# The scan's step-row fetches issued by ScalarE, next to the decay that frees their slot, with the positions of the steps set anew

## The chip, the cores and the metric

One core of one Trainium2 chip. The metric is the device time of one execution in microseconds (us). The kernel before took 2951.22 us (median of three runs, 2949.57 to 2960.09).

## What is computed

Two transformer layers with adaptive layer norm run over 32 samples of 256 tokens and 128 features. The reference, cut to what matters:

```python
# layer 0: attention with relative positions, then a mixture of 16 experts, 4 of them per token
x = x + ga * attention(layernorm(x) * (1 + ca) + sa)
x = x + gb * experts(layernorm(x) * (1 + cb) + sb)
# layer 1: a state-space layer (256 channels, 16 states), then three matrices and a tanh
dt  = softplus(dt_low @ W_dt + b_dt)
dA  = exp(dt[..., None] * A)                                  # [b, t, 256, 16]
dBx = dt[..., None] * B_ssm[:, :, None, :] * x_conv[..., None]
h   = associative_scan(h_t = dA_t * h_(t-1) + dBx_t)          # over t
y   = einsum('btdn,btn->btd', h, C_ssm)
x = x + ga * ((y * silu(z) + D * x_conv) @ W_out)
h = layernorm(x) * (1 + cb) + sb
x = x + gb * tanh(h @ W @ A1 @ A2 + bias)
```

## The kernel before

Two samples form a pair (512 tokens), and there are 16 pairs. Each pair passes through four stages: attention (32 chunks), experts (16), scan (32 batches of 128 rows of channel and state) and the last matrices. The stages of different pairs overlap. All engines walk through one list of steps, from FIRST to LAST; a pair begins every STEPS = 128 steps. The table `AT` says at which step of a pair each piece of work stands in its engine's program (the suffix names the engine, `_sync` is SyncE's DMA queue). Positions are only an order within one engine; between engines semaphores decide. So an engine that waits holds up whatever stands behind it in its own program. Attention's pieces return every 4 steps, an expert's every 8, and a scan batch m of a pair stands at SCAN + 27m//8, that is every 3.4 steps from step 388 on.

What a scan batch is made of, for the steps in question:

- The scan's step size and its product with x_conv are stored from SBUF (tile `step`) to the HBM tensor `dt_rows` (`s_store_sync`, L1072 to L1075). A fetch (L1105, "work<-dt_rows") reads 16 channels of it back, repeated over 8 groups of partitions, 128 x 1024 floats or 512 KB, into one of four slots of `ring`. There are 16 fetches a pair (n = 0 to 15), issued by SyncE in four groups of four. Each fetch serves two batches, four batches apart.
- ScalarE's decay (L1118, "bank<-work,neg_a") makes exp of the first half of a slot into the one PSUM bank 6; it waits for the fetch and for the scan before it, which frees the bank.
- GpSimd's input (L1129) multiplies the second half of the slot with a row of B, out of `bc`; VectorE scans (L1135); GpSimd reads out with C (L1142); TensorE sums over states (L1154).
- A slot is free when both the decay and the input of the second batch that uses it are done. SyncE waits for that at L1102 and L1103 and then issues the next fetch. `dt_rows` must have been stored (semaphores `dt_out`).

SyncE's one queue carries everything: besides the fetches the spread of the keys (L564, "ke<-ke"), the scatter of the queries (L553 and L556, many small pieces, "q_all<-q_rows"), the experts' weights (stored at L828 after ScalarE's copy at L821, fetched at L836 as "w_bc<-w_rows_d" for GpSimd's L902), the rows of B and C (stored at L1062, fetched at L1083), and the output (L1238, "out<-x_b"), whose buffer VectorE overwrites two pairs later at L927.

On ScalarE the attention's exp (L597, "probs") and copy of the turned probabilities (L615, "probs_t") and the experts' tanh (L878) stand between the decays. TensorE's L580 are the scores, L607 the turns, L870 and L871 an expert's gate, L889 its up and L907 its down product.

Of the kernel before, what the change touches and what calls it, by code (L numbers as in the profile page):

```python
# [15 lines left out]
PAIRS = B // 2  # L16
# [32 lines left out]
RING = 4  # L49
# [18 lines left out]
def build(nc, dram, out, q_rows, w_rows_d, dt_rows, bc_rows):  # L68
    ctx = ExitStack()
    with ctx:  # L70
# [254 lines left out]
        def tokens(ap):  # L325
# [8 lines left out]
        FIRST, LAST = -102, STEPS * (PAIRS - 1) + 538  # L334
# [3 lines left out]
            a_out_tensor=[79, 144], a_out_scalar=[79, 145], s_end_vector=[448, 500],  # L338
            a_spread_sync=[[-28, -28, -12, 4], [20, 36, 52, 68]], a_scatter_sync=[[-22, 4], [37, 69]], x_a_sync=-100,
            x_res_sync=104, a_store_sync=-35, m_store_sync=178, m_fetch_sync=-11, s_rows_sync=377,  # L340
            s_rows_in_sync=[378, 380, 384, 386], s_store_sync=[372, 374], s_fetch_sync=-14, f_store_sync=534,
            a_scores_tensor=0, m_gate_tensor=1, m_up_tensor=3, m_down_tensor=9, a_turn_tensor=5, a_values_tensor=40,
            a_inverse_tensor=42, s_sum_tensor=6, a_turned_tensor=-48, a_keys_tensor=-42, a_values_in_tensor=-37,
            a_query_tensor=-33, f_end_tensor=531, a_back_tensor=150, b_turned_tensor=159, m_logits_tensor=164,
            m_weights_tensor=178, m_back_tensor=326, s_turned_tensor=340, s_in_x_tensor=[348, 356], s_step_tensor=[364, 365],
            s_rows_tensor=374, s_in_z_tensor=[390, 397], f_out_tensor=508, f_back_tensor=513, f_turned_tensor=524,
            f_mix_tensor=527, s_decay_scalar=0, m_tanh_scalar=2, a_turn_scalar=8, a_exp_scalar=3, a_values_scalar=42,
            a_norm_scalar=-51, a_turned_scalar=-42, a_keys_scalar=-40, a_values_in_scalar=-35, a_query_scalar=-33,
            b_norm_scalar=156, b_turned_scalar=159, m_logits_scalar=166, m_weights_scalar=180, m_end_scalar=324,
            s_norm_scalar=340, s_turned_scalar=342, s_conv_scalar=[351, 359], s_step_scalar=[366, 366], s_rows_scalar=373,  # L350
# [743 lines left out]
        def last_batch_of(n):  # L1094
            return 8 * (n // 4) + 4 + n % 4

        def s_fetch_sync(sp, p, n):
            sp.wait_ge(dt_out[n // 8], (n // 8 + 1) * 16 * (p + 1))
            at = FETCHES * p + n - RING
            if at >= 0:  # L1100
# [594 lines left out]
```

## Time and profile before

| | us |
|---|---|
| median of three runs | 2951.22 |
| lowest and highest run | 2949.57, 2960.09 |
| the profiled execution's own time | 2962.1 |
| its span in the trace | 2960.3 |
| TensorE busy | 2429.2 (82%) |
| GpSimd busy | 1826.6 (62%) |
| VectorE busy | 1898.4 (64%) |
| ScalarE busy | 1633.4 (55%) |
| DMA packets' share of 16 engines | 51.9% |

Engines: PE is TensorE, PEld its weight loads, DVE VectorE, ACT ScalarE, POOL GpSimd, SP SyncE; SPq is SyncE's queue of DMA issues. The time of an issue in the timeline is how long the issuing instruction took, not the transfer. "a <-b" means that engine a sat idle until b. The span has a fill (to about 520 us), a stretch in which all four stages run side by side (560 to 2210 us is taken for it here, ten pairs), and a drain (from about 2450 us) in which the last pairs' scans are nearly alone.

### The profile page before, as it was taken

Reading aid. Unit: us, or ns where it says so; the run is one execution under the profiler, and the core shown is the slowest. Engines: PE = TensorE matmul, PEld = TensorE weight load, DVE = VectorE, ACT = ScalarE, POOL = GpSimd, SP = SyncE. Lnnn points to the kernel's source line nnn. Section 1 sums busy time; section 2 is a strip of 40 time slices with the busy share of each in tenths; the row PEclk is TensorE's granted clock in tenths of the full one; section 3 lists DMA queues with packets and bytes.
Section 4 is the critical chain, followed back from the end, with each engine's and each line's share of the span. In section 5 each row is a group of like instructions: output and inputs, shape, how many; then the busy total and the mean of one; then the engine's idle time right before and its main releaser. Section 6 shows DMA issues by size and latency. Waiting matters only on the chain.

```text
span 2960.3 us, 37054 instructions
## 1 busy us (share of the span) xinstructions
PE 2429.2 (82%) x9792; PEld 1231.4 (42%) x9792; DVE 1898.4 (64%) x3116; ACT 1633.4 (55%) x4152; POOL 1826.6 (62%) x2311
## 2 busy tenths in 40 slices
PE   2889988989898898989898888989898898867422
PEld 2555544444444444444444444444444444312100
DVE  2344557676767767676767767676767767565533
ACT  1655555656566666556566666666566656423322
POOL 2011248575767758575757767575758667675865
PEclk9999999999999999999999999999999999978655
DMA  5324355565655566565656655555656554434241
GB/s 123 45 44 73 57 123 99 118 109 120 114 100 122 102 131 104 112 106 118 115 109 114 106 122 111 115 109 109 118 111 119 106 112 94 115 86 109 70 108 43
DMA packets 495421, 304.95 MB, mean 103 GB/s; under 512 B 347258, under 2 KB 413738, under 8 KB 494762
## 3 DMA queue, kind: packets, MB, share of 16 engines
q1 hardware_dynamic: 495212, 302.58, 51.9%
q8 instruction: 82, 1.34, 0.2%
q14 instruction: 127, 1.03, 0.2%
HBM read 242.21 MB, written 26.74 MB: 91 GB/s over the span
## 4 chain that ended last, share of the span: by engine, by line
PE 37%; DVE 19%; issue 14%; POOL 11%; DMA 9%; ACT 7%; SPq 1%; DVEq 0%; ACTq 0%; POOLq 0%
PE bank L580 7%; DMA work<-dt_rows 7%; PE bank L889 6%; PE bank L871 4%; DVE work L1135 4%; POOL work L1142 4%; POOL work L1129 3%; PE bank L1154 3%; DVE zh L885 2%; PE bank L607 2%; PE bank L1007 2%; DVE step L981 2%; PE bank L907 2%; DVE nmax L587 2%; PE bank L682 2%
## 5 line engine op out<-in xcount | busy, mean ns | idle before, releaser
L1129 POOL TENSOR_TENSOR work<-work,bc 128x512 f32<-128x512 f32 x512 | 655.0, 1285 | 250.2 <-DMA work<-dt_rows 140.4
L1135 DVE TENSOR_TENSOR_SCAN work<-bank,work 128x512 f32<-128x512 f32 x512 | 621.7, 1214 | 215.1 <-POOL work L1129 161.6
L1142 POOL TENSOR_TENSOR work<-work,bc 128x512 f32<-128x512 f32 x512 | 659.1, 1293 | 115.5 <-DVE work L1135 113.8
L902 POOL TENSOR_TENSOR zh<-zh,w_bc 128x512 f32<-128x512 f32 x256 | 325.2, 1270 | 482.4 <-DVE zh L895 475.7
L1118 ACT ACTIVATE bank<-work,neg_a 128x510 f32<-128x510 f32 x512 | 353.0, 689 | 478.9 <-DVE work L1135 367.0
L597 ACT ACTIVATE probs<-bank,nmax 128x256 f32<-128x256 f32 x1024 | 474.9, 471 | 216.8 <-DVE nmax L587 215.9
L580 PE MATMUL bank<-ke,q_all 96*128 96x256 f32 x2048 | 560.9, 398 | 17.9 <-DMA q_all<-q_rows 17.9
L580 PEld LDWEIGHTS bank<-ke,q_all 96*128 96x128 f32 x2048 | 385.5, 198 | 227.2 <-issue 161.7
L587 DVE TENSOR_REDUCE nmax<-bank 128x2 f32<-128x512 f32 x512 | 347.1, 678 | 189.7 <-PE bank L580 180.1
L889 PE MATMUL bank<-h_b,w_t 128*128 128x512 f32 x512 | 299.4, 668 | 128.5 <-DVE zh L885 120.0
L607 PEld LDWEIGHTS bank<-ident,probs 128*128 128x128 f32 x2048 | 256.8, 146 | 287.1 <-issue 211.3
L607 PE MATMUL bank<-ident,probs 128*128 128x128 f32 x2048 | 323.2, 282 | 62.3 <-ACT probs_t L615 61.9
L615 ACT ACTIVATE probs_t<-bank 128x512 f32<-128x512 f32 x512 | 304.7, 595 | 98.5 <-PE bank L637 80.2
L885 DVE SCALAR_TENSOR_TENSOR zh<-th,bank 128x512 f32<-128x512 f32 x256 | 174.1, 680 | 220.8 <-ACT th L878 220.1
L895 DVE SCALAR_TENSOR_TENSOR zh<-bank,b_c,zh 128x512 f32<-128x512 f32 x256 | 190.9, 746 | 193.9 <-PE bank L889 192.6
L871 PE MATMUL bank<-h_b,w_t 128*128 128x512 f32 x512 | 310.6, 691 | 0.0
L907 PE MATMUL bank<-zh,w_t 128*128 128x512 f32 x512 | 282.9, 636 | 3.8 <-POOL zh L902 3.8
L878 ACT ACTIVATE th<-bank 128x512 f32<-128x512 f32 x256 | 152.3, 595 | 147.0 <-PE bank L871 144.2
L1154 PE MATMUL bank<-work,sel_d 128*32 128x512 f32 x1024 | 166.9, 689 | 77.5 <-POOL work L1142 77.5
L597 ACT ACTIVATION_READ_ACCUMULATOR probs<-bank,nmax 128x1 f32 x1024 | 206.9, 202 | 0.0
L889 PEld LDWEIGHTS bank<-h_b,w_t 128*128 128x128 f32 x512 | 81.1, 196 | 248.1 <-DVE zh L885 213.1
L907 PEld LDWEIGHTS bank<-zh,w_t 128*128 128x128 f32 x512 | 102.3, 203 | 146.4 <-issue 135.3
(190 smaller groups left out, 2509.1 us busy)
## 6 DMA issues: line engine op xcount, KB each, us to landing
work<-dt_rows SPq DMA_DIRECT2D x256, 512.0 KB
w_bc<-w_rows_d SPq DMA_DIRECT2D x256, 256.0 KB, 9.4
ke<-ke SPq DMA_DIRECT2D x128, 256.0 KB, 8.7
bc<-bc_rows SPq DMA_DIRECT2D x64, 256.0 KB
x_in<-in_x SPq DMA_DIRECT2D x32, 256.0 KB, 6.2
q_all<-q_rows SPq DMA_DIRECT2D x512, 8.0 KB
dt_rows<-step SPq DMA_DIRECT2D x16, 512.0 KB, 2.9
dt_rows<-step SPq DMA_DIRECT2D x32, 256.0 KB, 2.2
```

The lines of the kernel that those rows point to most:

```text
L580: last = nc.tensor.matmul(bank[n % 2][:, k * T:(k + 1) * T], q_all[0:QROWS, i0 + k, :], ke_q[:, i0 + k, :], start=True, stop=True)
L587: nc.vector.tensor_reduce(nmax[:, 2 * c:2 * c + 2], bank[n % 2][:, :].rearrange("p (k t) -> p k t", k=2), AX_X, ALU.max, negate=True).then ...
L597: last = nc.scalar.activation(probs[:, n % 2, k, :], bank[n % 2][:, k * T:(k + 1) * T], ACT.Exp, bias=nmax[:, i:i + 1], accum_out=rsum[:, ...
L607: last = nc.tensor.transpose(tile(bank[2], 2 * kh + k), probs[:, n % 2, k, kh * P:(kh + 1) * P], ident[:, :])
L871: nc.tensor.matmul(bank[4][:, :], w1_t[:, e, :], h_b[:, p % 2, :], start=False, stop=True).then_inc(m_g, 1)
L889: nc.tensor.matmul(bank[4][:, :], w3_t[:, e, :], h_b[:, p % 2, :], start=True, stop=True).then_inc(m_u, 1)
L902: nc.gpsimd.tensor_tensor(zh[:, n % 3, :], zh[:, n % 3, :], w_bc[:, n % WB, :], ALU.mult).then_inc(m_p, 1)
L907: nc.tensor.matmul(bank[5][:, :], w2_t[:, e, :], zh[:, n % 3, :], start=False, stop=(e == NE - 1)).then_inc(m_w2, 1)
L1118: nc.scalar.activation(segments(bank[6][:, :])[:, :, 1:], segments(ring[n % RING][:, 0, :])[:, :, 1:], ACT.Exp, scale=neg_a[:, SG * j + s: ...
L1129: nc.gpsimd.tensor_tensor(hb[at % HB], ring[n % RING][:, 1, :], bc[:, s, :], ALU.mult).then_inc(s_dbx, 1)
L1135: nc.vector.tensor_tensor_scan(hb[at % HB], bank[6][:, :], hb[at % HB], 0.0, ALU.mult, ALU.add).then_inc(s_h, 1)
L1142: nc.gpsimd.tensor_tensor(hb[at % HB], hb[at % HB], bc[:, SG + batch(m)[2], :], ALU.mult).then_inc(s_hc, 1)
```

## The change

SyncE no longer issues the fetches. ScalarE does, as `s_fetch_scalar`, with the same waits and the same transfer. In ScalarE's program the fetch for batch m stands at step 12 before that batch's decay, one or two steps behind the decay (of batch m - 4) that is the last reader of its slot; on SyncE it stood 14 steps before. Nearly every position of the table is set anew too, most by one or two steps; the larger moves are `m_weights_scalar` (180 to 187), `f_store_sync` (534 to 573), `x_res_sync` (104 to 114), `s_norm_scalar` (340 to 332), `a_turn_tensor` and `a_turn_scalar` (one later), and `s_step_scalar` (366 to 364 and 365).

```diff
-        FIRST, LAST = -102, STEPS * (PAIRS - 1) + 538
+        FIRST, LAST = -98, STEPS * (PAIRS - 1) + 577
...
-            s_rows_in_sync=[378, 380, 384, 386], s_store_sync=[372, 374], s_fetch_sync=-14, f_store_sync=534,
+            s_rows_in_sync=[378, 380, 384, 386], s_store_sync=[371, 375], f_store_sync=573, a_scores_tensor=0, m_gate_tensor=1,
...
-        def s_fetch_sync(sp, p, n):
-            sp.wait_ge(dt_out[n // 8], (n // 8 + 1) * 16 * (p + 1))
+        def s_fetch_scalar(act, p, n):
+            act.wait_ge(dt_out[n // 8], (n // 8 + 1) * 16 * (p + 1))
             at = FETCHES * p + n - RING
             if at >= 0:
                 done = BATCHES * (at // FETCHES) + last_batch_of(at % FETCHES) + 1
-                sp.wait_ge(s_dbx, done)
-                sp.wait_ge(s_da, done)
+                act.wait_ge(s_dbx, done)
+                act.wait_ge(s_da, done)
             j = ORDER[n]
-            sp.dma_start(ring[n % RING].rearrange("p r t -> p (r t)"),
+            act.dma_start(ring[n % RING].rearrange("p r t -> p (r t)"),
...
-            at = batch_due(AT["s_fetch_sync"], st)
-            if at is not None and at[1] % 8 < 4:
-                s_fetch_sync(sp, at[0], batch(at[1])[0])
...
             at = batch_due(AT["s_decay_scalar"], st)
             if at is not None:
                 s_decay_scalar(act, *at)
+            at = batch_due(AT["s_fetch_scalar"], st)
+            if at is not None and at[1] % 8 < 4:
+                s_fetch_scalar(act, at[0], batch(at[1])[0])
```

ScalarE's program in the steady stretch, before: the decays (L1118) of batches 14, 15 and 16 of a pair; L821 is the copy of the experts' weights.

```order
L1118 ACTIVATE bank<-work,neg_a 128x2x255 [waits s_h,s_in2]
L597 ACTIVATE probs,rsum<-bank,nmax 128x256 [waits a_t,a_max]
L597 ACTIVATE probs,rsum<-bank,nmax 128x256
L615 ACTIVATE probs_t<-bank 128x512 [waits a_t]
L821 ACTIVATE ke<-bank 32x512 [waits m_out,m_w2,m_wt]
L1118 ACTIVATE bank<-work,neg_a 128x2x255 [waits s_h,s_in3]
L597 ACTIVATE probs,rsum<-bank,nmax 128x256 [waits a_t,a_max]
L597 ACTIVATE probs,rsum<-bank,nmax 128x256
L615 ACTIVATE probs_t<-bank 128x512 [waits a_t]
L1118 ACTIVATE bank<-work,neg_a 128x2x255 [waits s_h,s_in0]
```

The same place now:

```order
L1118 ACTIVATE bank<-work,neg_a 128x2x255 [waits s_h,s_in2]
L597 ACTIVATE probs,rsum<-bank,nmax 128x256 [waits a_t,a_max]
L597 ACTIVATE probs,rsum<-bank,nmax 128x256
L1105 DMA work<-dt_rows 128x1x1024 [waits s_da,s_dbx,dt_out1]
L615 ACTIVATE probs_t<-bank 128x512 [waits a_t]
L1118 ACTIVATE bank<-work,neg_a 128x2x255 [waits s_h,s_in3]
L597 ACTIVATE probs,rsum<-bank,nmax 128x256 [waits a_t,a_max]
L597 ACTIVATE probs,rsum<-bank,nmax 128x256
L1105 DMA work<-dt_rows 128x1x1024 [waits s_da,s_dbx,dt_out1]
L615 ACTIVATE probs_t<-bank 128x512 [waits a_t]
L1118 ACTIVATE bank<-work,neg_a 128x2x255 [waits s_h,s_in0]
```

Fetches 10 and 11 have come in, each between an exp and a turn's copy; the copy L821 is gone from here and now stands after the decay that waits for s_in0.

SyncE's queue at the same place, before: L828 stores the experts' weights, L836 fetches them, L564 is a spread of the keys, L553 and L556 a scatter of the queries.

```order
L836 DMA w_bc<-w_rows_d 128x512
L1105 DMA work<-dt_rows 128x1x1024
L828 DMA w_rows_d<-ke 16x512
L1105 DMA work<-dt_rows 128x1x1024
L564 DMA ke<-ke 32x8x256
L836 DMA w_bc<-w_rows_d 128x512
L1105 DMA work<-dt_rows 128x1x1024
L836 DMA w_bc<-w_rows_d 128x512
L564 DMA ke<-ke 32x8x256
L836 DMA w_bc<-w_rows_d 128x512
L553 DMA q_all<-q_rows 8x16x16 x2
```

And now:

```order
L836 DMA w_bc<-w_rows_d 128x512
L828 DMA w_rows_d<-ke 16x512
L564 DMA ke<-ke 32x8x256
L836 DMA w_bc<-w_rows_d 128x512 x2
L1238 DMA out<-x_b 128x4x128
L564 DMA ke<-ke 32x8x256
L836 DMA w_bc<-w_rows_d 128x512
L553 DMA q_all<-q_rows 8x16x16 x2
```

The fetches are gone from the queue, and the output store L1238 has come in behind the weights' first two fetches.

## Rows read from the trace of the kernel before

**Rows 1.** Stretches: us, then busy us and count of each engine
```profile
560.00:2210.00 1650.00, 1475.42 (x6100) 758.10 (x6098) 1168.87 (x1920) 1013.28 (x2589) 1132.94 (x1440) 0.96 0.59 113
```

**Rows 2.** Chain of waits by line, 560 to 2210 us, then 2450 to 2960 us
```profile
by line: issue 16.1%; PE bank L580 7.2%; DMA work<-dt_rows 6.7%; PE bank L889 6.0%; DVE work L1135 4.9%; PE bank L871 4.7%; DVE zh L885 2.6%; POOL work L1142 2.5%; PE bank L1154 2.5%; POOL work L1129 2.2%; DVE step L981 2.0%; PE bank L607 2
...
by line: issue 17.1%; DMA work<-dt_rows 12.3%; POOL work L1142 9.9%; POOL work L1129 7.0%; PE bank L889 5.0%; PE bank L1154 4.8%; DVE work L1135 3.5%; PE bank L1007 3.0%; PE bank L871 2.8%; DVE step L981 1.9%; DVE zh L885 1.9%; DMA bc_rows<
```

**Rows 3.** Waits, 560 to 2210 us: us in total, times, longest
```profile
ACT bank L1118 <- DVE work L1135: 165.4, 132, 5.9
...
POOL work L1129 <- DMA work<-dt_rows: 88.0, 38, 5.2
...
ACT bank L1118 <- DMA work<-dt_rows: 38.4, 21, 3.1
...
PE bank L607 <- ACT probs_t L615: 30.7, 23, 2.8
```

**Rows 4.** Waits of SyncE's queue, 560 to 2210 us
```profile
SPq L1103 <- POOL work L1129: 93.7, 10, 9.6
SPq L1103 <- ACT bank L1118: 81.2, 34, 5.6
...
SPq L828 <- ACT ke L821: 27.3, 10, 4.2
```

**Rows 5.** Timeline of SyncE's issues: start us, us the issue took, operation
```profile
1788.23 0.32 SPq L828 DMA_DIRECT2D w_rows_d<-ke  x1
1788.65 0.60 SPq L1105 DMA_DIRECT2D work<-dt_rows  x1
...
1790.22 0.40 SPq L836 DMA_DIRECT2D w_bc<-w_rows_d  x1
1790.73 0.59 SPq L1105 DMA_DIRECT2D work<-dt_rows  x1
```

**Rows 6.** Timeline of ScalarE there; in brackets the idle time before
```profile
1787.62 0.58 ACT L821 ACTIVATE ke<-bank 32x512 f32<-32x512 f32 x1
1789.83 0.69 ACT L1118 ACTIVATE bank<-work,neg_a 128x510 f32<-128x510 f32 x1 [1.63 <-DVE work L1135]
...
1802.05 0.20 ACT L597 ACTIVATION_READ_ACCUMULATOR probs<-bank,nmax 128x1 f32 x1
1804.92 0.69 ACT L1118 ACTIVATE bank<-work,neg_a 128x510 f32<-128x510 f32 x1 [2.67 <-DMA work<-dt_rows]
```

**Rows 7.** Timeline of GpSimd there
```profile
1797.66 1.27 POOL L1129 TENSOR_TENSOR work<-work,bc 128x512 f32<-128x512 f32 x1 [0.46 <-DMA work<-dt_rows]
...
1804.97 1.26 POOL L1129 TENSOR_TENSOR work<-work,bc 128x512 f32<-128x512 f32 x1 [3.13 <-DMA work<-dt_rows]
...
1808.65 1.26 POOL L902 TENSOR_TENSOR zh<-zh,w_bc 128x512 f32<-128x512 f32 x1
```

**Rows 8.** Timeline of TensorE there
```profile
1806.27 1.09 PE L607 MATMUL bank<-ident,probs 128*128 128x128 f32 x4 [2.43 <-ACT probs_t L615]
```

**Rows 9.** Timeline of ScalarE in the drain
```profile
2855.84 0.69 ACT L1118 ACTIVATE bank<-work,neg_a 128x510 f32<-128x510 f32 x1 [1.42 <-DVE work L1135]
...
2866.37 0.69 ACT L1118 ACTIVATE bank<-work,neg_a 128x510 f32<-128x510 f32 x1 [4.18 <-DMA work<-dt_rows]
2870.61 0.69 ACT L1118 ACTIVATE bank<-work,neg_a 128x510 f32<-128x510 f32 x1 [3.54 <-DMA work<-dt_rows]
```

**Rows 10.** One line's issues each: count, ns least/median/most, first and last start
```profile
L1105 SPq DMA_DIRECT2D work<-dt_rows x256: 574/597/2152, 380.1 to 2906.1; - x128
...
L553 SPq DMA_DIRECT2D q_all<-q_rows x512: 265/358/9360, 54.1 to 2478.6; - x171
```

**Rows 11.** DMA issues by tile: count, KB each, median us from issue to landing
```profile
w_bc<-w_rows_d SPq DMA_DIRECT2D x256, 256.0 KB, 9.4
...
out<-x_b SPq DMA_DIRECT2D x16, 256.0 KB, 12.5
```

**Rows 12.** Pieces of the chain of waits in the drain: start us, us, what
```profile
2691.88 1.61 DMA bc_rows<-ke
...
2819.47 5.99 DMA bc_rows<-ke
```

More of the change, by code:

```diff
@@ new lines, in build @@
+            a_out_tensor=[79, 144], a_out_scalar=[82, 145], s_end_vector=[447, 499],
+            a_spread_sync=[[-28, -28, -12, 4], [20, 36, 52, 68]], a_scatter_sync=[[-22, 4], [37, 69]], x_a_sync=-96,
+            x_res_sync=114, a_store_sync=-32, m_store_sync=177, m_fetch_sync=-11, s_rows_sync=377,
+            s_rows_in_sync=[378, 380, 384, 386], s_store_sync=[371, 375], f_store_sync=573, a_scores_tensor=0, m_gate_tensor=1,
+            m_up_tensor=3, m_down_tensor=9, a_turn_tensor=6, a_values_tensor=40, a_inverse_tensor=42, s_sum_tensor=6,
@@ new lines, in build @@
+            a_turned_tensor=-47, a_keys_tensor=-42, a_values_in_tensor=-39, a_query_tensor=-35, f_end_tensor=531,
+            a_back_tensor=150, b_turned_tensor=160, m_logits_tensor=165, m_weights_tensor=177, m_back_tensor=326,
+            s_turned_tensor=340, s_in_x_tensor=[348, 356], s_step_tensor=[364, 365], s_rows_tensor=375,
+            s_in_z_tensor=[389, 397], f_out_tensor=512, f_back_tensor=513, f_turned_tensor=524, f_mix_tensor=527,
+            s_decay_scalar=0, m_tanh_scalar=2, a_turn_scalar=9, a_exp_scalar=3, a_values_scalar=41, a_norm_scalar=-50,
@@ new lines, in build @@
+            a_turned_scalar=-44, a_keys_scalar=-41, a_values_in_scalar=-37, a_query_scalar=-33, b_norm_scalar=158,
+            b_turned_scalar=162, m_logits_scalar=166, m_weights_scalar=187, m_end_scalar=326, s_norm_scalar=332,
+            s_turned_scalar=343, s_conv_scalar=[353, 359], s_step_scalar=[364, 365], s_rows_scalar=376, s_z_scalar=[391, 399],
+            f_out_scalar=512, f_turned_scalar=526, f_norm_scalar=525, f_mix_scalar=527, s_scan_vector=1, a_max_vector=1,
+            m_up_vector=4, m_silu_vector=2, a_inverse_vector=34, a_scale_vector=43, a_stats_vector=-88, a_end_vector=149,
@@ new lines, in build @@
+            b_stats_vector=152,
+            m_route_vector=[166, 166, 167, 167, 168, 168, 169, 169, 170, 170, 171, 171, 172, 172, 173, 173, 174, 175, 175, 175, 175],
+            m_end_vector=327, s_stats_vector=328, s_conv_vector=[[349, 349, 350, 350], [359, 359, 360, 360]],
+            s_silu_vector=[352, 360], s_zgate_vector=[391, 400], f_res_vector=518, f_stats_vector=518, f_end_vector=532,
+            s_read_gpsimd=4, m_weigh_gpsimd=5, s_input_gpsimd=-3, a_root_gpsimd=-83, b_root_gpsimd=152, s_root_gpsimd=330,
@@ L359, in build @@
+            f_root_gpsimd=519, s_step_vector=[367, 371], s_fetch_scalar=-12,
         )
```

20 lines of the change are left out of this document (removed).

## Prediction, written before the changed kernel was run

> **What bounds the kernel now.** I read the stretches first, then the chain of waits, the waits by total, and last the timelines of one place. In the steady stretch, 560 to 2210 us, ten pairs pass in 1650 us (SyncE's L828, which stands once per pair, waited ten times [rows 4]), so a pair costs 165 us. TensorE is busy for 1475.4 us of it, 147.5 a pair, ScalarE for 101.3 [rows 1]. The period is therefore TensorE's work plus 17.5 us of TensorE idling, and only what shortens that idling shortens the period. ScalarE idles 63.7 us a pair: room for more work, as long as nobody waits just then.
>
> The chain of waits shows what lies in the gaps. Transfers "work<-dt_rows" hold 6.7% of the steady chain (110 us, 11 a pair) and 12.3% of the drain's [rows 2]. By total, GpSimd waited 88.0 us for them (8.8 a pair) and ScalarE's decay 38.4 (3.8 a pair) [rows 3]. How that reaches TensorE is seen at one place. SyncE issues fetch 11 of a pair at 1790.73 [rows 5]. GpSimd and ScalarE both get going at 1804.9 only, after 3.13 and 2.67 us of idling [rows 6, 7]. Behind ScalarE's decay stands the turn's copy L615, and TensorE idles 2.43 us for it until 1806.27 [rows 8]. That line pair (L607 after L615) totals 30.7 us over the ten pairs, longest 2.8 [rows 3], so nearly all of it can be this place, once a pair. The transfer took 14.2 us from its issue, though in the drain, with little beside them, fetches queued up land one every 4.2 us (decays released at 2866.37 and 2870.61 [rows 9]). So most of the 14 us is queueing: fetch 10, issued at 1788.65, had released GpSimd at 1797.66 [rows 5, 7], and fetch 11 could have followed 4.2 us later, at 1801.9, before ScalarE came to wait at 1802.2.
>
> **The fetches leave SyncE's queue.** This is the gain. Two parts. First, SyncE stood at L1103 for 93.7 + 81.2 = 175 us over ten pairs [rows 4], 17.5 a pair, with scatters, spreads and weights behind it. What it frees is early for most: I price it at nothing on the path in the steady stretch. Second, the fetches no longer stand in line behind the transfers that SyncE issued before. The price at the place above: 2.4 us of TensorE idling a pair. Its bounds are 0 (the data travel no sooner) and 8.8, all that GpSimd waited for fetches. At the other places TensorE mostly had work while GpSimd waited, so I add 0.8 of the remaining 6.4 and take 3.2 us a pair.
>
> A rule speaks against this. The Trainium skill, "DMA: Bandwidth & Descriptors", section "Issuing engines are not separate DMA queues", says that DMAs from different issuing engines run on the same 16 DMA engines and interleave, and that a second issuer saves only the issuing time. By that rule alone the transfer's own time stays, and the gain would be nearly none. The same page's "Queues, rings and completion order" says that SyncE and ScalarE own separate rings between which each DMA engine takes turns by packets, by which a fetch would pass the backlog. No row of before has two issuers, so none decides between them.
>
> **ScalarE issues them.** This is the cost. Sixteen issues a pair at 0.60 us (median, least 0.57, most 2.15 [rows 10]) are 9.6 us a pair of ScalarE's program. No row shows an issue on ScalarE. Lower bound: 0, since the issue follows an ACTIVATE of 0.47 to 0.69 us that may still run meanwhile. Upper bound: all 9.6 us on the path. The order shows most fetches right behind an exp and ahead of a turn's copy, which TensorE awaits. I take half a cover, near 3 us of ScalarE's time a pair, and a third of that on the path, because ScalarE idles 63.7 of 165 us: 1.0 us a pair. In the drain each decay waits 1.42 us for the scan anyway [rows 9], more than the 0.6 of an issue, so it costs nothing there.
>
> **The new wait.** The fetch waits on ScalarE for GpSimd's input of batch m - 4. Queued behind are exps, turns' copies and tanhs, and TensorE waits for these. But the very next decay already waits for the scan of that batch, which needs the same input (132 such waits, 165.4 us, 16.5 a pair [rows 3]); the fetch only brings the wait forward by one or two attention pieces. Price 0 to 2 us a pair; I take 0.3, since GpSimd stands on the other side and is helped by earlier data.
>
> **Issue time of the fetch.** It stands two steps later (165/128 = 1.29 us a step, 2.6 us). Against that, SyncE issued many only when the slot came free. At the place shown the decay that frees the slot ends at 1790.52, SyncE issues at 1790.73 [rows 5, 6]; ScalarE would issue after the two exps, at about 1791.5, 0.8 us later. The fetch must then land in 10.7 us instead of 14.2 for the full gain.
>
> **The positions.** Two of them eat a margin. The copy of the experts' weights (L821) stands 7 steps later, 9.0 us. Before, it started at 1787.62 and the first user, GpSimd's L902, at 1808.65 [rows 6, 7], 21.0 us. Now 12.0 are left. Needed: 2.6 to the first fetch L836 (1790.22 [rows 5]) and 9.4 to land [rows 11], 12.0 in all. The output store stands 39 steps later, 10 steps or 12.9 us before VectorE overwrites its buffer at L927, and needs 12.5 [rows 11]. Both just fit, at before's landing times; a miss costs 1 to 3 us a pair. The other moves are within two steps or on engines with idle time. I put all positions at +0.2 us a pair, with bounds of -2 and +3.
>
> **The drain.** There the row of four fetches is limited by their own 4.2 us each, on whichever ring. One thing gains: the store of B and C's rows took 5.99 us in the last pair, behind a fetch, against 1.61 in an earlier one [rows 12], and GpSimd's first input waits for what follows it. With the fetch on another ring I take 4 us, and 3 more for the pairs before.
>
> **The sum.** Per pair -3.2 + 1.0 + 0.3 + 0.2 = -1.7 us; the scan runs beside everything else in about 14 pairs: -24 us. Drain -7. Together -31. The profiled execution (2962.1, span 2960.3) lies 11 us above the median of the runs shown, 2951.2, and the difference is carried over: 2951 - 31 = **2920 us**.
>
> **The rivals.**
>
> Hidden either way (0.20): the data move no sooner, because fetches and scatters share the same DMA engines, or another wait follows at once. For it: DMA packets are a share of 0.59 of 16 engines in the steady stretch [rows 1]. Against: 14.2 us against 4.2 apiece. The gain of 3.2 falls to about 1.2 a pair, the cost of 1.5 stays: +4 us less 4 in the drain, 2951.
>
> ScalarE's issues are held up (0.18): SyncE's scatter issues take 0.36 us in the median but up to 9.36 [rows 10], because what takes them in is full. If that place is shared, a ScalarE issue beside a scatter stalls too. The third and fourth groups of fetches and the first one's end stand beside scatters; four of sixteen fetches, 3.5 us each, are 14 us of ScalarE a pair. A third reaches TensorE: 4.7, of which the 1.7 gained is to be taken off, so +3.0 a pair, 42 us in 14 pairs: 2993. It decides from about 5 us of such stalls a pair. The fetch's own issues on SyncE, 2.15 at most, speak mildly against it.
>
> The positions miss (0.10): weights and store both land late, +3 a pair on top of a gain of 1.7: +18 us, 2969.
>
> Larger gain (0.14): all of GpSimd's fetch waits go and the period follows by 6 a pair net of cost: 2951 - 84 + rest, about 2870.
>
> The change does what it says by the order: all 256 fetches stand in ScalarE's program and none in SyncE's.
>
> **How the numbers follow.** Forecast case 0.38, around 2920 (2900 to 2936); larger gain 0.14; hidden 0.20; held up 0.18; positions 0.10. A measurement of this kernel tells about 0.5% from no change, 15 us. Faster by more: 0.38 + 0.14 = 0.52. Within: 0.20. Slower: 0.18 + 0.10 = 0.28. The range that leaves out a tenth at each end is 2872 to 2995. The likeliest side's own range is 2872 to 2936.
>
> **What would show it.** Right: in the steady stretch GpSimd's wait for "work<-dt_rows" well under 8.8 us a pair, ScalarE's under 3.8, the idle before L607 at this place gone, and a period near 163.3 us. An issue on ScalarE of 0.6 us with idle of at most 0.3 behind it. Wrong: issues on ScalarE of several us beside L553 and L556 (held up); waits of L902 for w_bc or of L927 for out<-x_b (positions); the fetch waits unchanged (hidden); TensorE waiting for q_all, if fetches now crowd out the scatter.

## The result and the profile after

The changed kernel takes 2977.53 us (median of 14 runs, 2960.13 to 2984.87), the kernel before in the same series 2952.38 (14 runs). The ratio is 1.008, its 95% interval 1.0064 to 1.0096: 25 us slower, where 31 us faster was forecast. The range of 2872 to 2995 holds the time, the direction is wrong.

First the waits between engines in the same stretch, 560 to 2210 us, to be read against [rows 3] (total us, times, longest):

```profile
ACT bank L1118 <- DVE work L1135: 196.9, 109, 8.3
...
POOL work L1129 <- DMA bc<-bc_rows: 109.3, 10, 12.4
...
PE bank L637 <- DVE x_b L1194: 47.8, 10, 6.3
...
PE bank L607 <- ACT probs_t L615: 13.4, 24, 1.2
```

What the change aimed at has happened. Over the whole run the fetches are waited for by ScalarE for 35.5 us and by GpSimd for 19.4 (the last two lines of the view of line L1105 below); before, the same view has 110.6 and 140.4. TensorE's wait for L615 fell from 30.7 to 13.4 us. But a wait that the prediction did not name now stands high on the list: GpSimd's first input of a pair waits for "bc", the row of B, 10.9 us a pair. In the kernel before the same view has

```profile
POOL work L1129 <- DMA bc<-bc_rows: 35.4, 10, 4.2
```

3.5 us a pair. Behind GpSimd's input stand the scan, then ScalarE's decay, whose longest wait grew from 5.9 to 8.3 us, and L1194, for which TensorE now waits 4.8 us a pair.

ScalarE's issue of a fetch, and who waited for one (whole run):

```profile
L1105 ACTq DMA_DIRECT2D work<-dt_rows x256: 581/582/1160, 380.0 to 2920.4; - x128
...
who waited for it (us, times):
  ACT bank L1118: 35.5, 17
  POOL work L1129: 19.4, 14
```

The issue takes 0.58 us, never more than 1.16.

Waits of SyncE's queue, 560 to 2210 us, against [rows 4]:

```profile
SPq L828 <- ACT ke L821: 160.6, 10, 22.6
...
SPq L1083 <- DMA bc_rows<-ke: 44.3, 9, 5.9
```

L1103 is gone from it, L828's wait for the weights' copy rose from 27.3 to 160.6 us (the copy stands later, and SyncE now arrives early), and L1083, the fetch of B's and C's rows, waits 4.4 us a pair for their store L1062 to land (before, 4.8 us in all ten pairs together).

Now the place itself. SyncE at the start of one pair's scan, before:

```profile
1709.84 0.34 SPq L1062 DMA_DIRECT2D bc_rows<-ke  x1
1710.29 0.64 SPq L1105 DMA_DIRECT2D work<-dt_rows  x1
1711.48 1.25 SPq L1083 DMA_DIRECT2D bc<-bc_rows  x2
1712.84 0.57 SPq L1105 DMA_DIRECT2D work<-dt_rows  x1
```

SyncE at the same place, after, and below it ScalarE's issues there, with the exp beside the first:

```profile
1709.65 0.33 SPq L1062 DMA_DIRECT2D bc_rows<-ke  x1
1715.99 1.37 SPq L1083 DMA_DIRECT2D bc<-bc_rows  x2
```

```profile
1707.61 0.47 ACT L597 ACTIVATE probs<-bank,nmax 128x256 f32<-128x256 f32 x1 [2.79 <-DVE nmax L587]
1707.69 0.60 ACTq L1105 DMA_DIRECT2D work<-dt_rows  x1
...
1711.55 0.58 ACTq L1105 DMA_DIRECT2D work<-dt_rows  x1
...
1712.85 0.58 ACTq L1105 DMA_DIRECT2D work<-dt_rows  x1
```

And GpSimd, before and after:

```profile
1719.30 2.51 POOL L1129 TENSOR_TENSOR work<-work,bc 128x512 f32<-128x512 f32 x2 [3.01 <-DMA bc<-bc_rows]
```

```profile
1728.51 2.48 POOL L1129 TENSOR_TENSOR work<-work,bc 128x512 f32<-128x512 f32 x2 [12.41 <-DMA bc<-bc_rows]
```

The store L1062 is issued at the same moment in both, 1709.8 and 1709.7. Before, the first of the four fetches of this group had been issued at 1702.9, one stood right behind the store, and the rows of B and C were fetched 1.6 us after the store, ahead of fetch 2 (1712.84) and fetch 3: SyncE's one program gave that order. After, fetches 0, 1 and 2 (1.5 MB) are issued by ScalarE at 1707.7, 1711.6 and 1712.9, on both sides of the small store and all ahead of the fetch that depends on it. That fetch is issued 6.3 us after the store and has landed by 1728.5, 12.5 us after its issue; before it took 7.8. Together GpSimd starts the pair's scan 9.2 us later.

So the delay has two halves of 4.7 us each. The second goes with the order: fetch 2 is now ahead of the rows, as fetch 1 was already. The first is a matter of time: fetch 0 now enters 2.0 us before the store and not 6.9. The views of the DMA queues (q1 is SyncE's, q10 ScalarE's; packets, MB, share of 16 engines) show how it holds the store up. First the changed kernel in 1709.6 to 1711.1, 1711.1 to 1713.3 and 1713.3 to 1715.2 us, then the kernel before in 1709.8 to 1711.6:

```profile
q1 hardware_dynamic: 24, 0.03, 8.5%
```

```profile
q10 hardware_dynamic: 64, 0.26, 49.9%
```

```profile
q1 hardware_dynamic: 24, 0.03, 9.0%
```

```profile
q1 hardware_dynamic: 48, 0.07, 14.7%
```

In the kernel before all 48 packets of the store go within these 1.8 us. After, 24 go at once. Then only the fetch's packets move for 2.2 us, in 49.9% of the capacity of 16 engines, that is on 8 of them, and the store's other 24 follow when the fetch is through. A packet's times are in the trace for every pair: in each of the first fourteen pairs of the changed kernel 16 of the store's 32 pieces of 2 KB start within 1.5 us of its issue and the other 16 only 3 to 6 us after it. So the store passed on the engines that the fetch leaves free, and on the others it stood behind the fetch's whole share of 16 rows, though it came by another queue. Two queues are not needed for that: in the last pair of the kernel before, where SyncE issues fetch 0 1.4 us ahead of the store, the second 16 pieces start 4 to 5 us after the issue too (the 5.99 us of [rows 12]).

A second thing is new. In five of twelve pairs VectorE's L1163 takes 4.8 us instead of 0.75 to 1.8. VectorE, and GpSimd beside it:

```profile
1633.54 4.80 DVE L1163 SCALAR_TENSOR_TENSOR z_gate<-x_slots,d_par,z_gate 128x512 f32<-128x512 f32 x1
```

```profile
1632.84 1.28 POOL L1129 TENSOR_TENSOR work<-work,bc 128x512 f32<-128x512 f32 x1
1634.07 2.50 POOL L1142 TENSOR_TENSOR work<-work,bc 128x512 f32<-128x512 f32 x2
1636.52 1.26 POOL L1129 TENSOR_TENSOR work<-work,bc 128x512 f32<-128x512 f32 x1
1639.55 1.27 POOL L1142 TENSOR_TENSOR work<-work,bc 128x512 f32<-128x512 f32 x1 [1.76 <-DVE work L1135]
```

L1163 starts while GpSimd works without a pause, and ends 0.6 us after GpSimd's row of work ends (1637.8). Pairs with that stall take 168 to 171 us, the others 162 to 165; before, every pair took 164 to 167 (by the first scores L580 of each pair).

In the drain SyncE, and then GpSimd, after:

```profile
2829.11 0.32 SPq L1062 DMA_DIRECT2D bc_rows<-ke  x1
2835.59 2.62 SPq L1083 DMA_DIRECT2D bc<-bc_rows  x4
```

```profile
2848.00 3.71 POOL L1129 TENSOR_TENSOR work<-work,bc 128x512 f32<-128x512 f32 x3 [26.18 <-DMA bc<-bc_rows]
```

The store takes 6.5 us to the issue that waits for it, not less than the 5.99 of [rows 12], and the rows take 12.4 us more to land; before it was 5.9 (issued at 2825.48, GpSimd off at 2831.35). The time from the last pair's first scores to the end of the span grew from 583 to 595 us, which is the larger part of the 15 us by which the two profiled executions differ (2975.5 and 2960.3 us of span).

### The profile page after: what moved, and what is told of

Read it like the earlier page. It is cut to its first block, busy times and chain, and to the rows that moved or that the text cites. A ratio compares the mean times of both kernels' runs of the same rounds, so it can differ in the third digit from the quotient of the medians.

```text
span 2975.5 us, 37054 instructions
## 1 busy us (share of the span) xinstructions
PE 2399.6 (81%) x9792; PEld 1215.2 (41%) x9792; DVE 1917.9 (64%) x3116; ACT 1634.3 (55%) x4152; POOL 1824.1 (61%) x2311
## 4 chain that ended last, share of the span: by engine, by line
PE 30%; issue 28%; POOL 23%; DVE 12%; ACT 4%; DMA 1%; SPq 0%; POOLq 0%; DVEq 0%; ACTq 0%
POOL work L1129 7%; POOL work L1142 7%; PE bank L580 5%; POOL zh L902 4%; PE bank L889 4%; PE bank L871 3%; DVE work L1135 3%; PE bank L607 3%; PE bank L637 2%; DVE step L981 2%; PE bank L682 2%; PE bank L907 2%; PE bank L1154 2%; DVE nmax L587 2%; DVE zh L885 1%
## 5 line engine op out<-in xcount | busy, mean ns | idle before, releaser
L1129 POOL TENSOR_TENSOR work<-work,bc 128x512 f32<-128x512 f32 x512 | 652.3, 1280 | 230.4 <-DMA bc<-bc_rows 186.5
L902 POOL TENSOR_TENSOR zh<-zh,w_bc 128x512 f32<-128x512 f32 x256 | 326.6, 1276 | 566.7 <-DVE zh L895 560.1
L597 ACT ACTIVATE probs<-bank,nmax 128x256 f32<-128x256 f32 x1024 | 474.1, 470 | 277.6 <-DVE nmax L587 272.0
L1118 ACT ACTIVATE bank<-work,neg_a 128x510 f32<-128x510 f32 x512 | 352.2, 688 | 453.9 <-DVE work L1135 416.1
L580 PE MATMUL bank<-ke,q_all 96*128 96x256 f32 x2048 | 551.7, 393 | 16.6 <-DMA q_all<-q_rows 16.6
L580 PEld LDWEIGHTS bank<-ke,q_all 96*128 96x128 f32 x2048 | 380.5, 196 | 209.0 <-issue 144.3
L889 PE MATMUL bank<-h_b,w_t 128*128 128x512 f32 x512 | 297.0, 663 | 124.3 <-DVE zh L885 119.2
L615 ACT ACTIVATE probs_t<-bank 128x512 f32<-128x512 f32 x512 | 303.4, 593 | 118.6 <-PE bank L637 87.8
L607 PE MATMUL bank<-ident,probs 128*128 128x128 f32 x2048 | 322.1, 281 | 41.6 <-ACT probs_t L615 39.6
L607 PEld LDWEIGHTS bank<-ident,probs 128*128 128x128 f32 x2048 | 250.6, 145 | 236.7 <-issue 179.6
L871 PE MATMUL bank<-h_b,w_t 128*128 128x512 f32 x512 | 302.7, 674 | 0.0
L907 PE MATMUL bank<-zh,w_t 128*128 128x512 f32 x512 | 274.4, 618 | 4.9 <-POOL zh L902 4.9
L597 ACT ACTIVATION_READ_ACCUMULATOR probs<-bank,nmax 128x1 f32 x1024 | 206.2, 201 | 0.0
L637 PE MATMUL bank<-probs_t,v_s 128*32 128x512 f32 x1024 | 144.7, 689 | 63.2 <-DVE x_b L1194 63.2
```

Of the source, the lines that this page charges most:

```text
L580: last = nc.tensor.matmul(bank[n % 2][:, k * T:(k + 1) * T], q_all[0:QROWS, i0 + k, :], ke_q[:, i0 + k, :], start=True, stop=True)
L597: last = nc.scalar.activation(probs[:, n % 2, k, :], bank[n % 2][:, k * T:(k + 1) * T], ACT.Exp, bias=nmax[:, i:i + 1], accum_out=rsum[:, ...
L607: last = nc.tensor.transpose(tile(bank[2], 2 * kh + k), probs[:, n % 2, k, kh * P:(kh + 1) * P], ident[:, :])
L871: nc.tensor.matmul(bank[4][:, :], w1_t[:, e, :], h_b[:, p % 2, :], start=False, stop=True).then_inc(m_g, 1)
L889: nc.tensor.matmul(bank[4][:, :], w3_t[:, e, :], h_b[:, p % 2, :], start=True, stop=True).then_inc(m_u, 1)
L902: nc.gpsimd.tensor_tensor(zh[:, n % 3, :], zh[:, n % 3, :], w_bc[:, n % WB, :], ALU.mult).then_inc(m_p, 1)
```

## The experiments

Theory A: all of the loss comes from the first four fetches of each pair, which ScalarE issues before B's and C's rows have travelled. Theory B: two queues of large fetches, or ScalarE's issues, cost in general. Beside them stand the positions, which could gain or lose by themselves. Each ratio below is to the kernel before on the same chip (its medians there were 2950 to 2957 us), with its 95% interval.

### The move and the positions apart

The table of before with the fetches on ScalarE:

```diff
-            s_store_sync=[372, 374], s_fetch_sync=-14, f_store_sync=534,
+            s_store_sync=[372, 374], f_store_sync=534,
...
+            s_step_vector=[364, 368], s_fetch_scalar=-12,
```

> The table of before, word for word, with only the fetches moved to ScalarE (12 steps ahead of their decay). Theory A (the first four fetches of a pair, now on a ring of their own, crowd out the rows of B and C, on which GpSimd's first input waits): GpSimd's wait for bc grows here too, from 3.5 us a pair to 8 or more, while the wait for fetches falls from 8.8 to under 3; the two about cancel, 2940 to 2965 us. Theory B (the long VectorE instruction L1163, 4.8 us in five pairs of the changed kernel, comes from the new positions): none of these 4.8 us here. Rival (the positions are what lost, the move as such gains what was forecast): 2915 to 2930.

Measured: 3030.98 us, ratio 1.0262 (1.0236 to 1.0288), against an expected 2940 to 2965. The move alone loses three times what the whole change loses. GpSimd's wait for bc is there, the place as expected, the size not; the fetch waits are all but gone:

```profile
POOL work L1129 <- DMA bc<-bc_rows: 115.4, 10, 12.7
POOL work L1129 <- DMA work<-dt_rows: 13.0, 10, 2.4
```

The new table with the fetches on SyncE:

```diff
-            s_step_vector=[367, 371], s_fetch_scalar=-12,
+            s_step_vector=[367, 371], s_fetch_sync=-14,
```

> The table of the changed kernel, but the fetches stay on SyncE, 14 steps ahead. Theory A: the rows of B and C stand in SyncE's queue ahead of the third and fourth fetch again, GpSimd's wait for bc is about 4 us a pair; the kernel is at 2950 to 2975 with the fetch waits of before (about 9 us a pair). Rival (the positions alone lose the time): the wait for bc is over 8 us a pair without the move too, and the time is above 2975.

Measured: 3026.8 us, ratio 1.0247 (1.0222 to 1.0273). The positions alone lose as much, by another way:

```profile
POOL work L1129 <- DMA work<-dt_rows: 167.7, 56, 6.9
ACT bank L1118 <- DMA work<-dt_rows: 133.7, 48, 7.0
```

The fetches come later than before (88.0 and 38.4 us then [rows 3]), and SyncE stands 86.7 us at L828 for the weights' copy (27.3 before [rows 4]), with fetches behind it. Together the two halves of the change lose 25 us, each by itself about 75: each takes away part of what the other costs.

### The first four fetches

The changed kernel with the first four fetches of each pair on SyncE, as before; the other twelve stay on ScalarE (the first lines stand in SyncE's program, the last two in ScalarE's):

```diff
+            at = batch_due(-14, st)
+            if at is not None and at[1] < 4:
+                s_fetch(sp, at[0], batch(at[1])[0])
...
-            if at is not None and at[1] % 8 < 4:
+            if at is not None and at[1] % 8 < 4 and at[1] >= 8:
```

> The changed kernel, but the first four of each pair's 16 fetches are issued by SyncE again, 14 steps ahead; the other twelve stay on ScalarE. Theory A: GpSimd's wait for bc falls from 10.9 us a pair to about 4, the gap at the third chunk of attention from 14 to about 9 us, and the period by 4 to 6 us: 2977 - 14 x 4 to 6 gives 2895 to 2925. Rival (bc is late for SyncE's own waits, or another wait follows at once): bc wait or time unchanged, 2965 to 2980.

Measured: 2931.24 us, ratio 0.9906 (0.9879 to 0.9932): faster than both kernels, by undoing a quarter of the move. The time from the last pair's first scores to the end is 584 us again. The same split in the table of before:

> The table of before; the first four fetches of a pair on SyncE at -14 as before, the other twelve on ScalarE at -12. Theory A (all that the move costs is the first group's displacement of B's and C's rows): the third chunk's gap is back at 8 us instead of 16, the period falls from 170 to 161 to 164 us, the time from 3031 to 2900 to 2940, below the kernel before. Rival B (two queues of large fetches cost in general, wherever they stand): the gap of some other chunk grows and the time stays above 2980.

Measured: 2924.34 us, ratio 0.9913 (0.9887 to 0.9939).

```profile
POOL work L1129 <- DMA bc<-bc_rows: 37.3, 11, 3.9
...
POOL work L1129 <- DMA work<-dt_rows: 16.5, 10, 2.8
...
PE bank L607 <- ACT probs_t L615: 7.6, 13, 0.9
...
ACT bank L1118 <- DMA work<-dt_rows: 3.2, 4, 1.1
```

The wait for bc is that of the kernel before, and the fetch waits are gone. And its complement, only the first four on ScalarE (the lines of ScalarE's program):

```diff
-            if at is not None and at[1] % 8 < 4:
+            if at is not None and at[1] % 8 < 4 and at[1] < 8:
```

> The table of before; only the first four fetches of a pair on ScalarE at -12, the other twelve stay on SyncE at -14. Theory A: GpSimd waits about 11 us a pair for bc, the third chunk's gap is 16 us, and the fetch waits later in the pair stay as in the kernel before: 3020 to 3060. Rival B: near 2951 plus a quarter of the 75 us that all four groups cost, 2970.

Measured: 3055.08 us, ratio 1.0358 (1.0331 to 1.0385).

```profile
POOL work L1129 <- DMA bc<-bc_rows: 111.7, 10, 13.0
```

In the table of before the parts add up: the twelve give 26 us (0.87%), the first four cost 106 (3.58%), together 80, and all sixteen cost 77 (2.62%). Theory A holds for the loss of the move. A large general cost, as theory B has it, is ruled out; a smaller one, hidden under the gain of the twelve, is not (the halves below).

Is it that a second queue exists, or when the large fetches enter? The changed kernel with the first four on ScalarE, but four steps later:

```diff
+            for late in (0, 4):
-            at = batch_due(AT["s_fetch_scalar"], st)
-            if at is not None and at[1] % 8 < 4:
+                at = batch_due(AT["s_fetch_scalar"] + late, st)
+                if at is not None and at[1] % 8 < 4 and (at[1] < 4) == (late > 0):
```

> The changed kernel, all sixteen fetches on ScalarE, the first four of a pair four steps later (at -8; about 5 us). If it is the time at which the large fetches enter that displaces the small ones of B and C: GpSimd's wait for bc falls from 10.9 to under 5 us a pair, the third chunk's gap from 14 to 7 to 10, the time to 2900 to 2945, unless the first decay now waits for its own fetch (that would show as ScalarE's L1118 waiting for dt_rows at the start of each pair, 2 to 5 us). If it is the second queue as such, the wait stays above 9 us and the time at 2965 to 2985.

Measured: 2976.09 us, ratio 1.0095 (1.0062 to 1.0128), no better. But the loss has changed its place (the last line is of SyncE's queue):

```profile
POOL work L1129 <- DMA work<-dt_rows: 64.0, 26, 4.3
ACT bank L1118 <- DMA work<-dt_rows: 42.4, 21, 3.6
```

```profile
SPq L1083 <- DMA bc_rows<-ke: 12.2, 10, 1.2
```

The store is no longer held up: SyncE waits 1.2 us a pair for it and not 4.4, and issues the rows' fetch 1.6 us after the store in every pair but the last. So a second queue by itself does not delay it; fetch 0 just ahead of it does.

The third chunk of attention, in which TensorE's gap shows the late start of the scan, is shorter (8.6 us instead of 14.1, the mean of twelve pairs by the starts of L580), and the fourth longer (8.7 instead of 3.6), because now the fetches themselves are late. So the time of entry decides what is late, and at both of the two times tried on ScalarE something is. The wait for bc no longer stands in the list by name; 4.9 us a pair of idling before the same L1129 are without a releaser there, so how much of it is left is open.

### The weights' copy

The new table with the fetches on SyncE, and the copy L821 back at its old step:

```diff
-            b_turned_scalar=162, m_logits_scalar=166, m_weights_scalar=187, m_end_scalar=326, s_norm_scalar=332,
+            b_turned_scalar=162, m_logits_scalar=166, m_weights_scalar=180, m_end_scalar=326, s_norm_scalar=332,
```

> The new positions with the fetches on SyncE, and the copy of the experts' weights back from step 187 to 180. If the loss of the positions on SyncE's queue (3027) is SyncE standing at the weights' store L828 (8.7 us a pair) with fetches behind it: that wait falls under 3.5 us a pair, the fetch waits of GpSimd from 16.8 to about 9 a pair, the 17th chunk's gap from 12 to 6, the time to 2945 to 2970. If it is other positions: above 3000.

Measured: 2939.2 us, ratio 0.9965 (0.9946 to 0.9984). One number in the table, seven steps, costs 2.8% as long as the fetches stand behind L828 in SyncE's queue; all other new positions together gain a little. Once the fetches are elsewhere, the same number should cost nothing. The same edit in the kernel with the split, and in the changed kernel:

> The new positions, the first four fetches of a pair on SyncE, the other twelve on ScalarE, and the weights' copy L821 back from step 187 to 180. With the fetches on SyncE the late copy cost 88 us (3027 against 2939). If it did so only by standing before fetches in SyncE's queue, it costs little once twelve of them are gone: the time is within 12 us of 2931, at 2915 to 2935. If it also cost by GpSimd's L902 waiting for w_bc (14.5 us in ten pairs with the copy at 187), that is all it can give: 15 to 20 us. If it is the copy's place in ScalarE's program that costs: 2860 to 2900.

> The changed kernel with the weights' copy L821 back from step 187 to 180 and nothing else. The displacement of B's and C's rows is untouched: GpSimd waits 10 to 12 us a pair for bc. If the place of the copy matters only through SyncE's queue: 2955 to 2985, as the changed kernel. If the stalls of VectorE's L1163 (4.8 us in half of the pairs) come and go with it, the period is 163 or 170 throughout: 2930 or 3010.

Measured: 2936.28 us, ratio 0.9936 (0.9914 to 0.9958), against 0.9906 with the copy at 187; and 2983.91 us, ratio 1.0088 (1.0062 to 1.0113), against 1.008. Nothing is gained in either. Putting it still earlier, at 178, gives nothing either:

> As the kernel with the split and the copy at 180, but the copy at 178, right behind TensorE's transposes (177), so that the weights' store leaves SyncE up to 2.6 us earlier. If w_bc was still the last thing to be late: 5 to 15 us faster. If ScalarE then waits for VectorE's weights, with a decay behind it: 5 to 20 us slower.

Measured: 2939.84 us, ratio 0.9947 (0.9924 to 0.9969).

### VectorE's long instruction

L1163 reads two operands from SBUF while GpSimd works. By the Trainium skill, "SBUF — State Buffer", section "SBUF: two separate sides", a VectorE instruction with two SBUF inputs and a GpSimd instruction that reads SBUF take the same pair of ports, one of them for the whole instruction, and the other is fully blocked. To test it one operand was taken from PSUM; the kernel so leaves out the term D * x_conv, and one wait of TensorE is moved with it (not shown):

```diff
-            nc.vector.scalar_tensor_tensor(z_gate[:, h, :], x_conv(p, h), d_par[:, h:h + 1], z_gate[:, h, :],
+            nc.vector.scalar_tensor_tensor(z_gate[:, h, :], bank[7][:, :], d_par[:, h:h + 1], z_gate[:, h, :],
...
```

> The changed kernel, but L1163 reads the PSUM bank 7 in place of x_conv, so that the term D * x_conv of the scan's result is left out (and the sum's wait is for L1163 in place of L1161); same length, one SBUF operand in place of two. Theory B (L1163 with two SBUF operands stands still while GpSimd works without a pause): L1163 takes 0.7 to 0.8 us in every pair, and the pairs of 170 us become 163 to 165: five of them by 5 to 6 us, 2977 - 25 to 33 gives 2944 to 2952. Rival (the 4.8 us are a wait for something else, such as the scan's data): some L1163 still take over 2 us and the time stays at 2965 to 2980.

Measured: 2988.55 us, ratio 1.0096 (1.0064 to 1.0129): no gain. Groups of VectorE's instructions in 560 to 2210 us (busy us, mean ns), first the changed kernel, then this one:

```profile
L1163 DVE SCALAR_TENSOR_TENSOR z_gate<-x_slots,d_par,z_gate 128x512 f32<-128x512 f32 x20 | 37.9, 1897 | 0.7
L655 DVE TENSOR_TENSOR dg<-rinv,mask_d 128x512 f32<-128x512 f32 x39 | 37.4, 960 | 1.3
```

```profile
L655 DVE TENSOR_TENSOR dg<-rinv,mask_d 128x512 f32<-128x512 f32 x40 | 61.3, 1533 | 1.4
L1163 DVE SCALAR_TENSOR_TENSOR z_gate<-bank,d_par,z_gate 128x512 f32<-128x512 f32 x19 | 14.3, 751 | 0.7
```

With one SBUF operand L1163 takes 0.75 us every time. The 23.6 us that it saves have gone to L655, the next instruction with two SBUF operands, which is 23.9 us longer and takes 4.0 us in twelve of sixteen pairs (1.8 at most in the changed kernel). The rule of the page and the trace agree on who is blocked; the gain does not follow, and the block is seen to pass on to the next one of that kind.

### What an issue on ScalarE costs

The split in the table of before, each of the twelve fetches on ScalarE cut in two halves of 64 partitions (`parts` is 2, `w` 64):

```diff
-            act.dma_start(ring[n % RING].rearrange("p r t -> p (r t)"),
-                         dt_rows[...].broadcast_to([P // DC, DC, 2 * TOK])).then_inc(s_in[n % RING], 16)
+            for k in range(parts):
+                act.dma_start(ring[n % RING][w * k:w * (k + 1)].rearrange("p r t -> p (r t)"),
+                              dt_rows[...].broadcast_to([w // DC, DC, 2 * TOK])).then_inc(s_in[n % RING], 16)
```

> The table of before with the split (first four on SyncE, twelve on ScalarE, 2924), each of the twelve fetches issued as two halves of 64 partitions: the same bytes, twelve more issues a pair on ScalarE of near 0.58 us, 7 us of ScalarE's program. If an issue lies beside the ACTIVATE still running or in idle time, as the timeline suggests: within 12 us of 2924. By the price of the prediction (1.0 us a pair for sixteen), 0.75 a pair: 2930 to 2940. If every issue lies on the path, 7 us a pair: 3020 or more.

Measured: 3183.99 us, ratio 1.0778 (1.0741 to 1.0815). This is no price of an issue. The issues took 0.52 us each; what went wrong is the transfers:

```profile
POOL work L1132 <- DMA work<-dt_rows: 192.0, 60, 6.9
```

(L1132 is L1129, three lines lower.) The Trainium skill, "DMA: Bandwidth & Descriptors", section "Why a DMA increments its semaphore by 16 and not by 1", says that a transfer is spread over as many DMA engines as divide the slowest dimension of both its sides, 16 at most. The source of a fetch repeats over 8 groups, of a half over 4: 8 engines, and then 4. The page of the profile counts on ScalarE's queue q10 26112 packets for 192 fetches (136 each: 128 rows and 8 more) and 26112 for 384 halves (68 each: 64 and 4), which agrees with it. So do the shares of the 16 engines while only these transfers move: 49.9% for a whole fetch above, and for the halves (1008 to 1012 us) a quarter:

```profile
q10 hardware_dynamic: 78, 0.30, 25.1%
```

The measurement again, cut by columns, so that all 128 partitions take part in each (`w` is 512, `parts` is 2 for the last twelve fetches of a pair):

```diff
+            src = dt_rows[...].unsqueeze(0).broadcast_to([P // DC, DC, 2 * TOK])
+            dst = ring[n % RING].rearrange("p r t -> p (r t)")
+            for k in range(parts):
+                act.dma_start(dst[:, w * k:w * (k + 1)], src[:, :, w * k:w * (k + 1)]).then_inc(s_in[n % RING], 16)
```

> As the split in the table of before (2924), each of the twelve fetches on ScalarE issued as two halves of its columns, all 128 partitions each: the same bytes, twelve more issues a pair on ScalarE of near 0.55 us, 6.6 us of its program. If an issue costs the path next to nothing: within 12 us of 2924, plus what the halves cost by themselves, which the same halves on SyncE show. If issues cost what the prediction took: 9 us more (2933). If all of it lies on the path: 90 us more.

And the same halves in the kernel before, issued by SyncE:

> The kernel before with the last twelve fetches of each pair issued by SyncE as two halves of their columns. This is what the halves cost without ScalarE: twelve more issues on SyncE and smaller pieces. If the pieces travel as fast: 2951 to 2965. If smaller pieces slow the transfers: over 2990, and the same surplus is then to be taken off the kernel with halves on ScalarE.

Measured: on ScalarE 2929.66 us, ratio 0.99 (0.988 to 0.9921), against 0.9913 with whole fetches: twelve more issues a pair, and the time is the same within some 10 us. On SyncE 2897.54 us, **ratio 0.9799 (0.9781 to 0.9818)**, the fastest kernel of the study. Its waits in the same stretch (L1133 and L1122 are L1129 and L1118):

```profile
POOL work L1133 <- DMA work<-dt_rows: 19.6, 14, 2.8
...
PE bank L607 <- ACT probs_t L615: 12.4, 18, 1.1
ACT bank L1122 <- DMA work<-dt_rows: 4.0, 4, 1.8
```

The waits of [rows 3] that the change was about fall from 88.0 and 38.4 us to 19.6 and 4.0, with every fetch where it was, in SyncE's queue. What changed is the time of the transfers. The page's lines of the one queue, the kernel before and this one (packets, MB, share of 16 engines):

```profile
q1 hardware_dynamic: 495212, 302.58, 51.9%
```

```profile
q1 hardware_dynamic: 521324, 302.58, 48.7%
```

The same bytes in more packets took less time, 48.7% of 2895 against 51.9% of 2960: 126 us less of all 16 engines. Pieces of 2 KB went through faster than rows of 4 KB: by the packets' times on ScalarE's queue a row of 4 KB took 269 ns on average with whole fetches, and a piece of 2 KB 118 ns with halves. Why is open, and so is why this kernel is 32 us ahead of the same halves on ScalarE, in which the fetch waits are as small: the mean time from one pair to the next is 160.7 against 163.6 us, and the surplus lies in several chunks of attention (0.6 us in the 21st, 1.4 in the 22nd) without one wait that carries it.

This takes the price of an issue back into doubt. The halves alone gain 58 us on SyncE and nothing on ScalarE, so the twelve more issues there may cost something that faster transfers pay for. What the runs give is this: the move of the twelve fetches, which gains 26 us with whole fetches, loses 32 with halves, 2.3 us a pair in fourteen for 24 issues on ScalarE. How much of it is the issues was not tested.

## Why the prediction was wrong

**The step that failed** is the first term's remark on what SyncE frees: "What it frees is early for most: I price it at nothing on the path in the steady stretch." The step listed what stands behind the fetches on SyncE and asked whether it would come earlier. It did not ask what would now meet a fetch that it used to miss. Four of the sixteen fetches of a pair stand next to the store and the fetch of B's and C's rows, on which GpSimd, and with it the scan, waits anyway, 3.5 us a pair before. That wait was in the trace and not among the rows read. The price is not nothing: in the table of before the four cost 106 us, four times what the other twelve bring, and in the changed kernel, where the new positions take some of it back, some 50 (1.008 against 0.9906 with the four on SyncE). Without them the changed kernel is at 2931 us, near the forecast of 2920.

"Issue time of the fetch" missed the same thing from the other side. It looked at fetch 11 and found 0.8 us. Fetch 0 moved by 5.0 us against the store, to 2.0 us ahead of it.

**The fetches leave SyncE's queue**, the gain: right in kind, and about right in size for the twelve that are not at that place. Their fetch waits went, L607's idle time with them (30.7 to 7.6 us), and they gave 26 us; the sum for the whole change was 31. "Most of the 14 us is queueing" holds for the place shown: the 128 rows of 4 KB of fetch 11, issued at 1790.7, start between 1798.9 and 1803.7, so some 8 us passed before the first moved. Another queue was not the only remedy, though: with the queue as it was and the fetches in halves the waits fell as far.

**The rule set against the change** turned out the one to heed, though not by its own result. All DMAs run on the same engines and interleave, whoever issues them (the Trainium skill, "DMA: Bandwidth & Descriptors", section "Issuing engines are not separate DMA queues"). The prediction drew from it only that the gain might be nil. At the place above half of a 64 KB store stood behind one 512 KB fetch that another engine had issued, on the 8 DMA engines that both use: 6.3 us from store to fetch instead of 1.6.

**The drain**: the term of 7 us rests on the same error with its sign. "With the fetch on another ring I take 4 us": the store took 6.5 us instead of 6.0, and the fetch behind it 12.4 instead of 5.9. The 583 us from the last pair's first scores to the end grew by 12.

**The range and the chances**: that the range holds the time is luck. The move alone took 3031 us, far outside it, and the new positions took 54 us back for reasons that the prediction does not have. Its 0.28 for a slower kernel stood on held-up issues and on weights and store landing late, and neither came.

**ScalarE issues them**: an issue took 0.58 us. The price of 1.0 us a pair for sixteen is neither shown nor refuted: with halves the move to ScalarE costs 2.3 us a pair for 24 issues, from causes not told apart. **The new wait** was not measured by itself. **Held up** (0.18) fell: the longest issue is 1.16 us.

**The positions**: right that the margins of 12.0 us hold. L902 does not wait for w_bc in the changed kernel, whose fetch now takes 5.4 us to land in the median instead of 9.4 [rows 11]. But +0.2 us a pair describes neither part of the truth. By themselves the positions cost 73 us, 5 a pair in fourteen, nearly all of it through SyncE waiting at L828 with fetches behind it, a path that the prediction left out; beside the move they cost nothing in that way, and take back 54 of the 77 us that the move loses in the old table. Which of the other positions do that is open. In the changed kernel the third chunk's gap is 14.1 us and not 16.1, and the time after the last pair's first scores is 12 us shorter; with the split there is nothing to take back, and the new positions are worth nothing (0.9906 against 0.9913).

**VectorE's stall** was in no case of the prediction. It goes with the pairs that took 170 us instead of 163, but it is not shown to cost that time: the changed kernel with the weights' copy back at 180 has no L1163 over 3.2 us and pairs of 164 to 167 throughout, the one with the first four later has a stall of 4.8 once, and both are as slow as the changed kernel. The kernel with the PSUM operand cannot tell, since there the stall stands at L655. With the table of before L1163 took 1.8 us at most, with the fetches on ScalarE too, so the 4.8 us take the new positions; why in these pairs is open.

## What to carry to other kernels

When a transfer is moved to another queue, list the small transfers that shared its queue and are awaited, and look at each for who is now ahead, and by how many microseconds: one queue is also an order, a second one has none with it, and a small transfer issued 2 us behind a large one stood behind it here from either queue. Move only those fetches that meet nothing. Before moving a transfer that is waited for, try its own shape, since that was worth more here (2.0% against 0.9%) than any place for it. And a position on one engine is to be followed not only to its first user but to every queue that waits for it, with all that stands behind.

## What the runs showed of the hardware

- A DMA issue on ScalarE took 0.58 us in the median of 256, at most 1.16, and ran beside an ACTIVATE (L597 from 1707.61 to 1708.08, the issue from 1707.69 to 1708.29).
- A 64 KB store issued 2.0 us behind a 512 KB fetch of the other queue moved 24 of its 48 packets at once and 24 after the fetch, 6.3 us to the issue that waits for it instead of 1.6.
- A broadcast fetch of 512 KB from 8 groups carried 136 packets and kept 49.9% of 16 DMA engines busy, a half by partitions 68 and 25.1%, in a kernel 7.8% slower; the same bytes in rows of 2 KB instead of 4 KB took 126 us less of all 16 DMA engines.
- A VectorE instruction with two SBUF operands stood for up to 4.8 us beside an unbroken row of GpSimd instructions, longer than any one of them (1.3 us): the block can last over several.
